# Decoder layer on one core: the passage from self-attention to cross-attention in another order

## The reference

```
x = layernorm(x + self_attention(x))        # 4 heads, 100 keys, mask by a learned window
x = layernorm(x + cross_attention(x, ctx))  # 16 heads of 16, 361 keys a batch
x = layernorm(x + experts(x))               # top 2 of 8 experts
```

## Time and profile before

| | |
|---|---|
| median of 3 runs | 677.12 us |
| profiled execution, own time | 676.91 us |
| its span, first to last instruction | 675.0 us |
| busy: PE, DVE, ACT, POOL | 625.9, 379.2, 311.8, 293.4 us |
| mean granted TensorE clock | 0.979 |
| self-attention up to pair 7's projections | to 89.7 us |
| passage, until the first cross-attention score | to 118.43 us |
| first turn (i = -1) | to 131.12 us |
| turns 0 to 15 | to about 402 us |
| experts and end | to 675.0 us |

### The profile page before, as it was taken

How to read it: one execution, slowest core, us unless ns; L and a number is a source line. 1 busy time by engine, 2 the same in 40 slices (tenths; PEclk the granted TensorE clock), 3 DMA queues, 4 the chain that set the end, 5 groups by cost and what they waited for, 6 DMA issues and landing times.

```text
span 675.0 us, 16884 instructions
## 1 busy us (share of the span) xinstructions
PE 625.9 (93%) x5901; PEld 530.2 (79%) x5902; DVE 379.2 (56%) x1003; ACT 311.8 (46%) x805; POOL 293.4 (43%) x524
## 2 busy tenths in 40 slices
PE   6989885899999998999989989999999999999984
PEld 5888873567777776777767768899999999999984
DVE  2778784777777886678767967422222222222244
ACT  2444424377777776677767765222122221121214
POOL 3535354333363448534584343325343342435244
PEclk9999978799999999899999999999999999999999
DMA  8332103555665654344443338588666776666443
GB/s 251 104 83 70 54 26 93 153 151 169 215 186 174 189 175 116 101 129 125 119 119 105 104 121 289 194 288 232 206 205 218 236 232 205 207 203 232 138 129 136
DMA packets 72898, 109.37 MB, mean 162 GB/s; under 512 B 9786, under 2 KB 50562, under 8 KB 72066
## 3 DMA queue, kind: packets, MB, share of 16 engines
q1 hardware_dynamic: 66882, 100.40, 48.1%
q0 software_dynamic: 5952, 8.14, 5.4%
HBM read 73.77 MB, written 12.44 MB: 128 GB/s over the span
## 4 chain that ended last, share of the span: by engine, by line
PE 41%; DMA 20%; issue 12%; DVE 10%; POOL 7%; POOLq 6%; ACT 2%; SPq 2%; DVEq 0%; ACTq 0%
DMA accd<-y,si 16%; PE ps L1593 6%; PE ps L1645 6%; PE ps L1667 6%; PE ps L1620 5%; POOLq L726 5%; PE ps L1604 5%; PE ps L1653 2%; PE ps L1688 2%; PE ps L804 1%; PE ps L1513 1%; DMA xT_sb<-in_xT 1%; POOL r_ln L366 1%; POOL accd L720 1%; DVE a_mx L2125 1%
## 5 line engine op out<-in xcount | busy, mean ns | idle before, releaser
L2136 DVE TENSOR_REDUCE cmx<-ps 100x1 f32<-100x361 f32 x256 | 134.5, 531 | 70.8 <-PE ps L1593 66.6
L804 PE MATMUL ps<-xsT,W 128*128 128x128 f32 x1408 | 164.6, 275 | 2.3 <-DVE hT L994 2.3
L804 PEld LDWEIGHTS ps<-xsT,W 128*128 128x128 f32 x1408 | 160.5, 192 | 2.9 <-DVE hT L994 2.7
L1908 ACT ACTIVATE cpr<-ps 128x300 f32<-128x300 f32 x256 | 104.8, 420 | 58.0 <-PE ps L1604 57.4
L1593 PE MATMUL ps<-st 96*100 96x361 bf16 x256 | 86.2, 341 | 7.1 <-DMA st<-parts 3.8
L853 PE MATMUL ps<-WD,hT 128*128 x384 | 88.5, 380 | 2.4 <-DVE hT L997 1.8
L1604 PEld LDWEIGHTS ps<-st 120*128 120x128 bf16 x768 | 62.8, 102 | 32.1 <-issue 9.3
L1604 PE MATMUL ps<-st 120*128 120x100 bf16 x768 | 76.8, 208 | 3.5 <-ACT st L1913 1.6
L853 PEld LDWEIGHTS ps<-WD,hT 128*128 128x128 f32 x384 | 70.5, 190 | 11.3 <-issue 3.1
L1008 DVE TENSOR_SCALAR y<-ps,wt 128x256 f32<-128x256 f32 x28 | 13.5, 483 | 106.4 <-PE ps L853 106.4
L720 POOL DMA_INDIRECT accd<-y,si x28 | 45.0, 1606 | 64.2 <-DMA accd<-y,si 55.0
(11 more groups left out here) (267 smaller groups left out, 1029.3 us busy)
## 6 DMA issues: line engine op xcount, KB each, us to landing
W<-in_wgu SPq DMA_DIRECT2D x32, 1408.0 KB, 6.5
st<-parts SPq DMA_DIRECT2D x192, 115.2 KB, 2.5
WD<-in_wd SPq DMA_DIRECT2D x6, 1024.0 KB, 5.9
cx<-in_ctxT SPq DMA_DIRECT2D x16, 361.0 KB, 3.9
x_sb<-in_x SPq DMA_DIRECT2D x8, 200.0 KB
x1d<-x SPq DMA_DIRECT2D x8, 200.0 KB
x1Td<-x1T SPq DMA_DIRECT2D x8, 200.0 KB, 3.4
x1T_sb<-x1Td SPq DMA_DIRECT2D x16, 100.0 KB, 3.3
```

What stands on the lines that cost most here:

```text
L804: mm = pe.matmul(out[:, i * P:(i + 1) * P], self.columns(t, k, c), self.xsT[:, t.par, k, :], start=(k == 0), stop=(k == KC - 1))
L1908: act.activation(pr[:, h % (2 * HG), :], ps[:, B_T + h % 2, 0:NCH * L], ACT.Exp).then_inc(exp_ok, 1)
L2136: dve.tensor_reduce(mx[:, half, hh:hh + 1], ps[0:L, B_S + h % 2, 0:CTX], AX_X, ALU.max).then_inc(max_ok, 1)
```

## The change

Nothing is computed in another way; instructions change their places. The self-attention loops now end at `PAIRS - 1`, and what was in the `g == PAIRS` clauses is written out behind them or within pair 6.

- TensorE: `keys(0, 0)` moves from behind `scores(7)` to between the two halves of `turn_probs(6)`; `keys(1, 0)`, `queries(1)` and `keys(1, 1)` move from behind pair 7's values to around its two `turn_probs`; `turn_x1(7)` moves from ahead of the first turn to its head 8.
- VectorE: batch 0's parts stand ahead of, and between, the two halves of pair 7's softmax, and all of them ahead of pair 7's norm.
- ScalarE: pair 7's window exponential ahead of pair 6's second `a_exps`; batch 0's outputs ahead of pair 7's softmax; batch 1's between the pieces of pair 7's; `x1T_copy(5)`, `(6)` and `(7)` each later.
- GpSimd: `copy_first(0, 0)` ahead of `finish(6)`, `copy_first(0, 1)` behind it, then the bias copy `bvr`, then `finish(7)`.
- SyncE: `stack(0, *)` ahead of `a_store(6)` and `store_T(6)`; `a_store(7)` and `store_T(7)` behind `stack(1, *)`.

```diff
@@ SyncE @@
-                    if g == PAIRS:
+                    if g == PAIRS - 1:
                         stack(0, 0)
                         stack(0, 1)
...
                 load_x1T(2)
+                store_T(PAIRS - 2)
                 for i in ITER[1:]:
...
                         stack(i + 2, 1)
+                    if i < 0:
+                        a_store(PAIRS - 1)
+                        store_T(PAIRS - 1)
@@ GpSimd @@
                     add_bias(g)
-                    finish(g - 1)
+                    if g < PAIRS - 1:
+                        finish(g - 1)
+                copy_first(0, 0)
+                finish(PAIRS - 2)
+                copy_first(0, 1)
                 pool.wait_ge(cross_in, 16 * cross.LOADS)
                 pool.tensor_copy(bvr[:, :, :], bv_sb[:, :].unsqueeze(2).to_broadcast([P, KC, L])).then_inc(c_step, 1)
-                copy_first(0, 0)
-                copy_first(0, 1)
                 finish(PAIRS - 1)
@@ TensorE @@
+                    if g == PAIRS:
+                        pe.wait_ge(k_ev, 1)
+                        keys(1, 0)
                     if 1 <= g <= PAIRS:
-                        turn_probs(g - 1)
+                        turn_probs(g - 1, 0)
+                    if g == PAIRS - 1:
+                        pe.wait_ge(cross_in, 16 * cross.LOADS)
+                        pe.wait_ge(dx_ev, PAIRS)
+                        keys(0, 0)
+                    if g == PAIRS:
+                        pe.wait_ge(q_ev, 1)
+                        queries(1)
+                    if 1 <= g <= PAIRS:
+                        turn_probs(g - 1, 1)
+                    if g == PAIRS:
+                        pe.wait_ge(k_ev, 2)
+                        keys(1, 1)
...
+                        if h == 8 and i < 0:
+                            turn_x1(PAIRS - 1)
@@ ScalarE, behind the loop @@
+                keys_out(0, 0)
+                act.wait_ge(act_set, 2)
+                queries_out(0)
+                keys_out(0, 1)
+                second_part(0, 0)
+                x1T_copy(PAIRS - 3)
+                a_exps(PAIRS - 1, 0)
+                second_part(0, 1)
+                keys_out(1, 0)
+                a_exps(PAIRS - 1, 1)
+                probs_out(PAIRS - 1, 0)
+                queries_out(1)
+                probs_out(PAIRS - 1, 1)
+                keys_out(1, 1)
+                x1T_copy(PAIRS - 2)
@@ VectorE, behind the loop @@
+                first_part(0, 0)
+                rest(0, 0)
+                softmax_in(PAIRS - 1, (0,))
+                first_part(0, 1)
+                rest(0, 1)
+                third_part(0, 0)
+                softmax_in(PAIRS - 1, (1,))
+                third_part(0, 1)
+                a_normalise(PAIRS - 1)
```

More of the change, by code:

```diff
@@ L1287, in _ @@
                 cross.load(sp, cross_in)
-                for g in range(PAIRS + 2):
+                for g in range(PAIRS):
                     if g == 2:
@@ L1554, in scores, with turn_probs @@
                                 mm.then_inc(a_s_mm, 1)
[L1556 to L1562, removed]
+                def turn_probs(g, hp):
+                    pe.wait_ge(p_ok, 2 * g + hp + 1)
+                    for c in range(4):
+                        mm = pe.transpose(ps[0:L, a_B_S + hp, c * L:(c + 1) * L], a_pr[:, hp, c * L:(c + 1) * L],
+                                          ident[0:L, 0:L])
+                    mm.then_inc(pT_mm, 1)
                 def a_weigh_values(g):
@@ L1750, in _ @@
                     kq, s, t, tail = stages(i)
[L1751 to L1757, removed]
                     for h in range(H):
@@ L1970, in _ @@
                 act.wait_ge(wqkv_in, 32)
[L1971 to L1974, removed]
-                        act.wait_ge(cross_in, 16 * cross.LOADS)
-                        act.mul(bq4[:, :], bqk_sb[:, 0:KC], 1.0 / np.sqrt(DH)).then_inc(act_set, 1)
-                        keys_out(0, 0)
-                    if 1 <= g <= PAIRS:
-                        a_exps(g - 1, 0)
-                    if g < PAIRS:
-                        qk_out(g, 1)
-                    if g == PAIRS:
-                        act.wait_ge(act_set, 2)
-                        queries_out(0)
-                    if 1 <= g <= PAIRS:
+                for g in range(PAIRS):
+                    qk_out(g, 0)
+                    if g >= 1:
+                        a_exps(g - 1, 0)
+                    qk_out(g, 1)
+                    if g == PAIRS - 1:
+                        window_out(g)
+                    if g >= 1:
                         a_exps(g - 1, 1)
-                    if g == PAIRS:
-                        keys_out(0, 1)
                     if g == 0:
@@ L1992, in _ @@
                         weff_out()
[L1993 removed]
+                    if g < PAIRS - 1:
                         window_out(g)
[L1995 to L1997 removed]
+                    if g > 0:
+                        v_out(g)
+                    if g >= 1:
                         probs_out(g - 1, 0)
@@ L2001, in _ @@
                         projections(g + 1)
-                    if g == PAIRS:
-                        second_part(0, 0)
-                        second_part(0, 1)
-                    if g >= 2:
+                    if 2 <= g < PAIRS - 1:
                         x1T_copy(g - 2)
+                act.wait_ge(cross_in, 16 * cross.LOADS)
+                act.mul(bq4[:, :], bqk_sb[:, 0:KC], 1.0 / np.sqrt(DH)).then_inc(act_set, 1)
+                keys_out(0, 0)
[13 more added lines that the diff above has]
+                x1T_copy(PAIRS - 2)
                 for i in ITER[1:-1]:
@@ L2011, in _ @@
                             exps(i, h)
-                        if h == 0 and kq:
+                        if h == 0 and kq and t:
                             keys_out(i + 2, 0)
-                        if h == 1 and kq:
+                        if h == 1 and kq and t:
                             queries_out(i + 2)
@@ L2017, in _ @@
                             weighed_out(i - 1)
-                        if h == 4 and kq:
+                        if h == 4 and kq and t:
                             keys_out(i + 2, 1)
-                        if h == 4 and i < 0:
+                        if h == 10 and i < 0:
                             x1T_copy(PAIRS - 1)
@@ L2110, in masks, with softmax_in @@
                     mk.then_inc(mask_ok, 1)
-                def softmax_in(g):
-                    for hp in range(2):
+                def softmax_in(g, halves=(0, 1)):
+                    for hp in halves:
                         n = 2 * g + hp
@@ L2186, in _ @@
                 dve.tensor_copy(cross.own_keys(0), cross.own_heads()).then_inc(own_rows_ok, 1)
-                for g in range(PAIRS + 1):
+                for g in range(PAIRS):
                     if g >= 1:
```

22 lines of the change are left out of this document (3 added, 19 removed).

## The result

The changed kernel took 673.54 us in the median of 20 runs, the kernel before 676.68 in as many. The medians are 3.1 us apart; the ratio of the runs compared is 0.9959, with a 95% interval of 0.9942 to 0.9977, which is a gain of 2.8 us where 8.0 were forecast. In a second comparison the ratio was 0.9950 [0.9925, 0.9975], 3.4 us. The time lies in the range, but the gain is 0.4% and so within what I had called no change.

What follows compares the result with a forecast made beforehand. One serial chain was taken to bound the passage: pair 7's softmax and norm, batch 0's parts, transfer. First maximum 8.1 us earlier, less 0.1 in the first turn, gave 8.0 us and 669.0 us; range 665.3 to 674.0.

Steps and rivals of the forecast that it cites:

- step 3: VectorE's batch 0 work beside GpSimd: one CAST held up, 0.6 us (bounds nothing to 1.2); third parts costed at nothing.
- step 4: Pair 7 through TensorE: norm ends at 110.1 us at full clock, 111.8 at half; 110.9 taken.
- step 6: First turn: first maximum at 110.9, 8.1 us earlier; 0.1 us lost in the turn, bounds 0.9 lost to 1.5 won.
- the sum: 119.01 - 110.9 = 8.1 us, less 0.1: 8.0 us gained, giving 669.0 us; bounds 666.1 and 671.4.
- Step 1: keys(0, 0) fills pair 6's 1.06 us gap, costing 1.41 us instead of 2.77; the clock fall at 93.3 us goes.
- Rival A: The clock falls at 93 us all the same: gain 5 to 6 us, 671 to 672.5; chance 0.20 for 671 to 674.
- Step 2: VectorE free at 96.7 us after pair 6's norm; 6.12 us of work, pair 7's second softmax half out at 102.8.
- Rival B: GpSimd blocks VectorE in full, 4.6 us more than counted for batch 0's parts: gain 3.4, 673.7 us; chance 0.07.
- my worst case: Both CASTs held up and clock at half: norm ends at 112.4; first turn loses 0.9; gain 5.7 us, 671.4.
- Step 5: Batch 0's half 0 transfer, ready at 101.7 us, lands at 109.3, some 1.6 ahead of the norm's end; DMA no bound.
- Rival C: Batch 1's scores become the new wait in front of turn 0: gain 0 to 3 us, 674 to 677; chance 0.07.
- Rival D: Half clock carried into turns 0 and 1: from 16 us at half the gain is gone, 30 us gives 684; chance 0.05.

Runs made afterwards that it cites:

- the fills: Matmuls nobody reads in TensorE's idle gaps: on the changed kernel 669.25 us against 676.95 for before; on the kernel before 673.75 against 677.06.
- The last experiment: Changed kernel with useless matmuls in TensorE's gaps and keys(1, 1) moved to head 1 of the first turn: 671.42 us, ratio 0.9892 to before.

## Why the prediction was wrong

The mechanism was right: the chain of softmax, norm, parts and transfer was cut as forecast. Its size was not: 8.0 us forecast, 4.1 won in the stretch and about 3 at the end. What failed are terms: in step 3 the third part, put at nothing; in step 4 the clock around pair 7, put at the middle; in step 6 the loss in the first turn, put at 0.1; and in the sum the 119.01 of one trace, taken for the kernel before. The 3.9 us between 8.0 and 4.1 are made up so.

**The sum: 1.4 us.** 49.69 us of before is 48.3 in the mean of its three profiles. I had read the fall at 93.3 as a property of the order; it comes in some runs of it only. Step 1 removes it where it would have come. Counted against the trace that I priced, which has it, the forecast was off by 2.6, not 3.9. This term is the least certain, since it hangs on one profile of three, and the priced execution as a whole, 676.91 us, was no slower than the median of its kernel.

**Step 1: right.** Full clock, keys at 1.45 us, the gap in front of the values 0.59 where I had 0.7. The wait of 1.06 us between the halves is gone. Rival A is refuted.

**Step 2: right.** By my times, shifted by the 3.58 us by which pair 5's values came later in this profile, VectorE should have been free at 100.28 and was so at 100.38.

**Step 3: half right, 0.6 us.** One CAST was held up and one not, 1.05 and 0.40, as booked. But the third part, whose delay I had costed at nothing, took 1.28 instead of 0.62 beside the x1 write. Pair 7's second softmax half was out at 107.69 instead of 106.98. The bound of 1.2 us held, the value taken did not. Of the two rows that I had taken as evidence, the one at 96.84 has its first operand in PSUM (`s<-ps,mask`), so it is of another kind than the third part, and only the subtraction at 99.76 was like it. The Trainium skill (SBUF — State Buffer, "Who interferes with whom") has an operation with two SBUF inputs contend with a GpSimd instruction that reads. The third part agrees, and so do the 0.98 and 1.01 us of the first turn, the 4.02 us of GpSimd where VectorE kept its pace, and the copy at 101.50, which took 1.26 us instead of 0.78 while the difference beside it kept its 0.64; the subtraction at 107.11, 0.58 us beside an x1 write that had started before it, does not, though it took 0.85 in the variant with finish(6) late. Rival B had the right place at over six times the price: 4.6 us, against 0.7 for the third part; another 0.6 came in the first turn, of which B did not speak.

**Step 4: 0.8 us.** I took the middle between full and half clock. It was half: the second turns took 0.91 us instead of 0.55, keys(1, 1) 2.66, and only the end of the values was at full clock. From keys(1, 1) to the maximum it took 7.01 us (109.02 to 116.03) instead of 6.4. The maximum less the shift, 116.03 - 3.58 = 112.45, is where I had put my worst case, 112.4. With the clock full, as with the fills, the first maximum came 29.0 us after pair 5's values, against 28.5 by my full-clock case, 110.1.

In the three profiles together steps 3 and 4 are 1.7 us.

**Step 5: right.** No DMA ended a wait in the passage of after. The stack was issued at 106.02, where I had 105.28 with the shift. The last experiment shows how far this holds: with the norm 2.1 to 2.5 us earlier the transfer was level with it.

**Step 6: 0.9 us.** I booked 0.1 lost, with 0.9 as the bound, and 1.0 was lost (12.27 against 13.23). At half clock turn_x1(7) costs 0.87 us inside the turn, VectorE's difference takes 0.98 beside finish(7), and its third part 1.01 beside the copy behind that, against 0.66 and 0.70 later in the turn. The clock is not the whole cause: with the fills it is full in the first turn of both orders, and the turn took 11.63 us in the old order and 12.45 in the new one. Rival C, a new wait for batch 1's stack, did not come. Rival D neither: the half clock ends 3.4 us ahead of turn 0, against 3.8 before.

**Behind turn 0: 0.8 us lost, unsettled.** From turn 0 to the end the six profiles give 542.0 to 544.3 for before and 543.8 to 544.8 for after; the variants give 541.4 to 543.2 with the same instructions there. A part of it goes with half-clock stretches of 3.4 or 6.8 us near 270, 340 and 655 us, which come in some profiles and not in others: the five of the fourteen profiles with 3.4 us in all give 541.4 to 543.2, the nine with more 542.6 to 544.8. One of the five is a profile of before and none is one of after. Whether that is chance three profiles of each do not show.

The forecast's 41.7 us for the stretch came out at 41.46 once the clock was full. That is in part luck, since the forecast had pair 7 at the middle of the two clocks and no delay of the third part, and the two errors point opposite ways. Read plainly, I had promised about what the new order gives with its clock held up.

## What to carry to other kernels

Before an edit is priced by a stretch at half clock, profile the unchanged kernel two or three times: the same gaps gave the fall in two profiles of three, and in the median an edit wins back no more than the usual run loses. When work is moved into a gap, ask what the gaps left behind do to the clock; 22 dummy matmuls in idle time were worth 2.8 us of the stretch here, beside 4.1 for the whole reordering. And a VectorE piece moved beside GpSimd's work should be booked at the slow price if it stands on the path.

## What the runs showed of the hardware

Identical instructions with like waits (1.07 and 0.88 us) were followed by full clock in one profile and by 6.8 us at 1.2 GHz in two, and the stretch took 46.1 us against 49.2 and 49.7. One TensorE piece in the first 22 us took 2.9 to 3.0 us in six profiles and 4.7 to 5.7 in eight, whichever kernel ran, and the later work started up to 4 us later with it. Beside GpSimd a two-input VectorE operation took 1.28 to 1.45 us instead of 0.62 to 0.70 in some places; in others it kept its pace and GpSimd paid, with 4.02 us instead of 2.74 for an x1 write and 1.26 instead of 0.78 for a copy; and the subtraction beside an x1 write took 0.58 us in one order and 0.85 in another.
